# Gate and up columns of an expert layer: loaded per block from DRAM in place of copied from resident weights

## What is computed

```
x = x + xattn0(ctx_2048, layernorm(x), mask)        # 8 heads, 77 keys
x = x + moe0(layernorm(x))                          # 8 experts, top 2, I = 704, and one shared expert, 352
x = x + depool1(layernorm(x), ctx_2048, lengths)    # W_in, norms, a decaying sum over 77 patches, picked per row
x = x + moe1(layernorm(x))                          # 32 experts, top 6, I = 128, and one shared expert, 512
# moe0, per expert: silu(h @ Wg) * (h @ Wu) @ Wd, weighted by the softmax of the two best logits
```

## Time and profile before

| | us |
|---|---|
| median of 3 runs | 851.08 (849.27 to 855.88) |
| the profiled execution | 853.57 |
| its span, first to last instruction | 851.8 |
| TensorE busy | 741.3 |
| VectorE busy | 480.9 |
| ScalarE busy | 276.9 |
| GpSimd busy | 308.7 |
| mean granted TensorE clock | 0.93 of full |

### The profile page before, as it was taken

One profiled execution on the slowest core, in us unless ns is written; L12 is line 12 of the kernel. 1 busy time (PEld: TensorE's weight loads), 2 busy tenths in 40 slices (PEclk: granted clock), 3 DMA queues, 4 the chain that ended last, 5 costly groups with the idle time before them and its releaser, 6 DMA issues.

```text
span 851.8 us, 14479 instructions
## 1 busy us (share of the span) xinstructions
PE 741.3 (87%) x4703; PEld 644.3 (76%) x4703; DVE 480.9 (56%) x1694; ACT 276.9 (33%) x625; POOL 308.7 (36%) x328
## 2 busy tenths in 40 slices
PE   4989999979999999999989965898690899998875
PEld 3777778979999999999979944666460777777664
DVE  4997875226555555555535448788600455567663
ACT  2644432211111111111111123443330466665530
POOL 1332323730111111101101100777776377776750
PEclk9996887999999999999999975999996799999998
DMA  8970037442433443444330354766433666688966
GB/s 257 424 241 1 1 101 313 158 137 84 114 104 115 125 118 104 112 125 120 103 105 13 102 168 136 223 215 208 150 120 115 210 214 216 218 307 297 322 218 239
DMA packets 74516, 141.72 MB, mean 166 GB/s; under 512 B 8838, under 2 KB 53979, under 8 KB 73091
## 3 DMA queue, kind: packets, MB, share of 16 engines
q1 hardware_dynamic: 59036, 99.21, 38.0%
q0 software_dynamic: 13344, 38.68, 12.1%
q10 hardware_dynamic: 2046, 2.71, 1.1%
HBM read 93.34 MB, written 66.89 MB: 188 GB/s over the span
## 4 chain that ended last, share of the span: by engine, by line
PE 53%; POOL 15%; DVE 14%; issue 10%; DMA 4%; ACT 2%; DVEq 1%; SPq 0%; POOLq 0%; ACTq 0%
PE PB L603 21%; PE PB L629 12%; POOL rows_in L1921 8%; PE PB L818 5%; POOL sorted_x L1887 4%; POOL rows_out L1933 3%; PE PB L829 2%; PE PB L528 2%; DMA X<-in_x 2%; DVE WK L1797 1%; PE PB L696 1%; PE PB L804 1%; PE PB L582 1%; DVE WK L1282 1%; PE PB L860 1%
## 5 line engine op out<-in xcount | busy, mean ns | idle before, releaser
L603 PE MATMUL PB<-XT,UPW 128*128 128x128 f32 x1584 | 184.6, 277 | 3.4 <-DVE UPW L1454 3.1
L603 PEld LDWEIGHTS PB<-XT,UPW 128*128 128x128 f32 x1584 | 181.3, 193 | 3.8 <-DVE UPW L1454 3.3
L1896 POOL DMA_INDIRECT sorted_y<-WK x36 | 34.4, 955 | 267.1 <-DVE WK L1488 267.1
L1921 POOL DMA_INDIRECT rows_in<-XR,MB x96 | 93.1, 970 | 81.8 <-DVE MB L1687 53.2
L1454 DVE COPY UPW<-BIG 128x1024 f32 x72 | 64.3, 894 | 63.3 <-PE PB L603 37.4
L629 PE MATMUL PB<-BIG,WK 128*128 x432 | 99.2, 379 | 0.0
L629 PEld LDWEIGHTS PB<-BIG,WK 128*128 128x128 f32 x432 | 79.3, 190 | 9.3
L818 PE MATMUL PB<-XTB,WK 128*128 128x128 f32 x456 | 65.6, 288 | 14.0 <-DVE WK L1797 12.4
L935 ACT ACTIVATE XT<-PB 128x256 f32<-128x256 f32 x52 | 20.0, 384 | 171.0 <-PE PB L582 171.0
L818 PEld LDWEIGHTS PB<-XTB,WK 128*128 128x128 f32 x456 | 56.9, 196 | 22.9 <-issue 16.2
L1933 POOL DMA_INDIRECT rows_out<-WS,MB x58 | 57.5, 991 | 35.4 <-ACT WS L1074 22.6
(11 more groups left out here) (271 smaller groups left out, 1258.1 us busy)
## 6 DMA issues: line engine op xcount, KB each, us to landing
rows_in<-in_consts SPq DMA_DIRECT2D x32, 600.0 KB, 5.3
R<-rows_in SPq DMA_DIRECT2D x58, 300.0 KB, 3.9
BIG<-in_w SPq DMA_DIRECT2D x4, 2176.0 KB, 20.4
W1E<-in_w SPq DMA_DIRECT2D x32, 256.0 KB, 3.1
BIG<-in_w SPq DMA_DIRECT2D x1, 6528.0 KB, 19.3
sorted_x<-BIG SPq DMA_DIRECT2D x1, 5070.0 KB, 42.6
WK<-sorted_x SPq DMA_DIRECT2D x36, 130.0 KB, 2.3
XR<-rows_out SPq DMA_DIRECT2D x6, 768.0 KB, 8.2
```

The lines of the kernel that those rows point to most:

```text
L603: t = e.matmul(o[:, to:to + P], UPW[m][n % (m + 1)][:, k, c * P:(c + 1) * P], XT[:, n % 2, k, :], start=(k == 0), stop=(k == 1))
L1896: e.indirect_dma_start(out=DY, out_offset=bass.IndirectOffsetOnAxis(ap=DEST[:, i:i + 1], axis=0), in_=YS[:, i % 2, :], in_offset=None).the ...
L1921: e.indirect_dma_start(out=DX1, out_offset=bass.IndirectOffsetOnAxis(ap=SLOT1[:, i, j:j + 1], axis=0), in_=XR[:, i, :], in_offset=None).th ...
```

## The change

- BIG goes. One tile MEM is cut by hand. DW holds the down weights of all eight experts, loaded once at the start in two DMAs.
- Gate and up columns of a block are loaded by SyncE from the DRAM tensor in_w0 into UPW0 (now three buffers) and UPW1 (now two), at an address made from a register with the block's expert. VectorE's copies go.
- The attention's tiles, XNA, and the patches have room of their own, so the late loads of experts 4 to 7 go, and so do the store and the reload of the patches; the second layer reads DPA and SELA where they were made.
- The 32 clears of rows_in are queued on SyncE right behind the zeroing of sorted_x, in place of one per block.

```
-            for j in range(4):
-                e.dma_start(BIG[:, j, :], w0[j]).then_inc(*q.land("in_w", j))
+            for j in range(2):
+                e.dma_start(DW[:, 4 * j:4 * j + 4, :],
+                            w0[4 * j:4 * j + 4, :, 4 * I0:WE].rearrange("e p c -> p e c")).then_inc(*q.land("in_dw", j))
             q.wait_ge("set", "zero")
             e.dma_start(DX.rearrange("(n p) d -> p n d", p=P), ZERO.unsqueeze(1).broadcast_to([P, NBLK, RW0])).then_inc(
                 *q.land("zeroed"))
-            q.wait_ge("dpa", 3)
-            q.wait_ge("in_bin")
-            e.dma_start(DS[0], DPA.rearrange("k b d -> k (b d)")).then_inc(*q.land("spill", 0))
-            q.wait_ge("sel", 3)
-            e.dma_start(DS[1], SELA).then_inc(*q.land("spill", 1))
-            q.wait_ge("st", NT - 1)
-            q.wait_ge("spill", 1)
-            q.wait_ge("zeroed")
-            e.dma_start(BIG[:, 5:8, :].rearrange("p e c -> p (e c)"), w0[5:8].rearrange("e p c -> p e c")).then_inc(
-                *q.land("in_w5"))
+            for k in range(32):
+                e.dma_start(DX1[1 + 4 * P * k:1 + 4 * P * (k + 1), :].rearrange("(n p) d -> p n d", p=P),
+                            consts[:, NC_:NC_ + RW].unsqueeze(1).broadcast_to([P, 4, RW])).then_inc(*q.land("clear", k))
...
+            regs = {}
+
+            def up_weights(i, m, nb):
+                if i < nb:
+                    q.wait_ge("tab")
+                    if i not in regs:
+                        regs[i] = e.value_load(TAB[0:1, i:i + 1], min_val=0, max_val=E0 - 1)
+                    q.wait_ge(f"up{m}", EARLY + i - 3 + m if i >= 3 - m else -1)
+                    lo, hi = ((0, 7 * P), (7 * P, 11 * P))[m]
+                    e.dma_start(UPW[m][i % (3 - m)],
+                                w0[bass.ds(regs[i], 1), :, 0:4 * I0].rearrange("e p (k c) -> p (e k) c", k=2)[:, :, lo:hi]
+                                ).then_inc(*q.land(f"uw{m}{i % (3 - m)}", i))
 
             def block_iteration(n, nb):
-                last = EARLY + nb - 1
-                if n + 3 <= last:
+                if n + 3 < EARLY + nb:
                     fetch(n + 3, nb)
-                if n + 1 < EARLY and ((n + 1) % 4 == 3 or n + 2 == EARLY):
...
+                i = n - EARLY
+                if i < -1:
+                    return
+                if i == -1:
+                    up_weights(0, 0, nb)
+                    up_weights(0, 1, nb)
+                    up_weights(1, 0, nb)
+                else:
+                    up_weights(i + 1, 1, nb)
+                    up_weights(i + 2, 0, nb)
...
-                    e.tensor_copy(UPW[m][n % (m + 1)][:], BIG[:, bass.ds(regs[i], 1), 0:4 * I0].rearrange(
-                        "p e (k c) -> p (e k) c", k=2)[:, :, lo:hi]).then_inc(*q.mark(f"wc{m}", n))
...
-                        q.wait_ge(f"wc{m}", n)
+                        q.wait_ge(f"uw{m}{i % (3 - m)}", i)
...
-                e.dma_start(R16[0:KV + 1, 0:2048], DS[0]).then_inc(*q.land("in_dp", 0))
-                e.dma_start(SELT, DS[1]).then_inc(*q.land("in_dp", 1))
```

More of the change, by code:

```diff
@@ L335, in build @@
         ident = CC[:, CI:CI + P]
-        one = ExitStack()
         WS = sb("WS", [P, WSH])
         WK = sb("WK", [P, 5152])
-        BIG = alloc(one, "BIG", [P, E0, WE])
-        UPW = [[alloc(one, f"UPW{m}{k}", [P, 2, (7 - 3 * m) * P]) for k in range(m + 1)] for m in range(2)]
-        ROOM = BIG[:, 5:8, :].rearrange("p e c -> p (e c)")
+        MEM = sb("MEM", [P, 38624])
+        DW = MEM[:, 0:E0 * 6 * D].rearrange("p (e c) -> p e c", e=E0)
+        UPW = [[MEM[:, a + k * w:a + (k + 1) * w].rearrange("p (k c) -> p k c", k=2) for k in range(3 - m)]
+               for m, (a, w) in enumerate(((12288, 14 * P), (17664, 8 * P)))]
+        R16 = MEM[:, 19712:23808]
+        ROOM = MEM[:, 23808:36904]
         CX = ROOM[0:KV, 0:4096].rearrange("k (b d) -> k b d", b=B)
         A = ROOM[:, 4096:8320]
-        DPA = ROOM[0:KV + 1, 8320:10368].rearrange("k (b d) -> k b d", b=B)
-        SELA = ROOM[0:KV + 1, 10368:12416]
-        MB = ROOM[:, 12416:13032]
+        XNA = ROOM[:, 8320:12480].rearrange("p (t d) -> p t d", t=NT)
+        MB = ROOM[:, 12480:13096]
+        DPA = R16[0:KV + 1, 0:2048].rearrange("k (b d) -> k b d", b=B)
+        SELA = R16[0:KV + 1, 2048:4096]
         SS = WK[:, 0:2 * NH * KV].rearrange("p (a h k) -> p a h k", a=2, h=NH)
@@ L602, in up @@
                             for k in range(2):
-                                t = e.matmul(o[:, to:to + P], UPW[m][n % (m + 1)][:, k, c * P:(c + 1) * P],
+                                t = e.matmul(o[:, to:to + P], UPW[m][i % (3 - m)][:, k, c * P:(c + 1) * P],
                                              XT[:, n % 2, k, :], start=(k == 0), stop=(k == 1))
@@ L696, in attend @@
                             e.matmul(o, XP(i)[:, c, :], WIN[:, c, :], start=(c == 0), stop=False)
[L697 to L698 removed]
+                        q.wait_ge("dpa", 3)
+                        q.wait_ge("sel", 3)
+                        q.wait_ge("in_bin")
+                        e.matmul(o, SELA[:, i * P:(i + 1) * P], DPA[:, i // 2, :], start=False, stop=True).then_inc(
                             *q.mark("wi", i))
@@ L1437, in target @@
                         *q.mark("to", n))
[L1439 to L1445, removed]
-                            for j in range(4):
-                                q.wait_ge("in_w", j)
-                            q.wait_ge("in_w5")
-                            q.wait_ge("in_w4", 3)
-                        q.wait_ge("tab")
-                        regs[i] = e.value_load(TAB[0:1, i:i + 1], min_val=0, max_val=E0 - 1)
-                    lo, hi = ((0, 7 * P), (7 * P, 11 * P))[m]
-                    q.wait_ge(f"up{m}", n - m - 1)
-                    e.tensor_copy(UPW[m][n % (m + 1)][:], BIG[:, bass.ds(regs[i], 1), 0:4 * I0].rearrange(
-                        "p e (k c) -> p (e k) c", k=2)[:, :, lo:hi]).then_inc(*q.mark(f"wc{m}", n))
             def hidden(n, nb):
                 kind, i = item(n, nb)
-                weights(n + 1, 0, nb)
                 q.wait_ge("sg", n)
@@ L1496, in block_iteration @@
                     target(n + 1, nb)
-                    weights(n + 1, 1, nb)
                 if n < count:
```

61 lines of the change are left out of this document (20 added, 41 removed).

## The result

| | before | after |
|---|---|---|
| median of 4 runs, us | 853.48 (849.27 to 856.78) | 840.07 (839.12 to 842.64) |
| the profiled execution, us | 853.57 | 839.12 |
| its span | 851.8 | 837.3 |
| TensorE busy | 741.3 | 733.1 |
| VectorE busy | 480.9 | 419.2 |

The ratio of the two times is put at 0.9873, 95% interval 0.9832 to 0.9915: the change makes the kernel 7 to 14 us faster. (The two medians above, 13.4 us apart, have a ratio of 0.984, inside that interval too.) The forecast was 848.3 with a range of 844 to 854.

A forecast was written before the change was run, and what follows sets the result against it. TensorE's matmuls were taken as the bound, with the removed copies beside a full engine. Block 0's 3.0 us off the 851.08 median gave 848.1, rounded for the seams to 848.3, the other parts at zero; range 844 to 854.

The forecast's parts named there:

- Block 0: First expert block: weight loads replacing VectorE's copies start it at 188.6 to 189.5, not 191.70; gain 3.0 us taken.
- The steady blocks: Expert blocks stay 7.72 us apart; weights, rows and results stream at 221 GB/s, costed at nothing.
- The clears' end: Clears queued on SyncE behind the zeroing of sorted_x during attention would end near 143 us.
- Attention's first ten tiles: Attention beside the moved clears: a saturated DMA slows it by zero, with 2 us either way.
- (a): Weight stream comes late, L603 waiting in every block: 29 us more at 200 GB/s, so 877 us; chance 0.09.
- (b): Clears outrun attention, ending at 224; block 0 would wait 42 us: 890 us; chance 0.03.
- part 3: Patches stay in SBUF, two stores and two loads of 624 KB go: nothing on the path, seams 0, ends +1 and -1.
- Rival (c): Code comes late at the 437.63 branch behind queued weights: 3.81 us become 5 to 8, 849 to 852; chance 0.12.
- rival (d): TensorE's granted clock moves: a microsecond's shift can make or spare a slow stretch, 843 to 853; chance 0.11.

The follow-up runs named there:

- second pair of traces: The kernel before and the changed kernel each traced once more with no edit: 844.46 us and 838.53 us.

## Why the prediction was wrong

**Right.** Block 0: forecast a gain of 2.2 to 3.1 us, 3.0 taken; measured 2.5 in the distance from the last scatter and 2.6 from the first (1.9 in the second pair of traces). It is at the lower part because TensorE was free 0.3 us later than forecast, behind a wait of 2.24 us for block 0's rows (1.69 before), and then stood 0.30 us for the first load, which took 4.5 us where the sum had 3.9. The steady blocks: 243.17 us to the jump in both kernels; share 0.70 against a forecast of 0.6, 223 GB/s against 221. The clears' end: 143 forecast, 140 to 144 seen. Attention's first ten tiles are not slowed by the clears (last section). Rivals (a) and (b) didn't come, though the clears alone, in the kernel before, showed what (b) looks like, at a price of 7.4 us.

**The step that failed** is the end of part 3: "1.25 MB less ahead of the first seam and a fuller DMA at the second could give or cost about 1 us each; I take 0 for the pair, +1 and -1 as ends." ("First" is there the end of the layer, 498.53, and "the second" the jump into the copy, 437.63.) Measured: the jump -2.9 us, the gate and up behind it -1.6 (this term was in no sum, although has it at 6.80 us for 4.91), the layer's end -2.3 us, with +0.9 given back before rows_in: -5.8 us (-5.6 in the second pair of traces). With block 0 that is 8.4 us (7.5), where 3.0 was forecast. 853.57 - 8.4 = 845.2, still inside the range; from the median of 851.08 it is 842.7, below the range's low edge and 1% faster. The measured 840.07 lies lower still, and the part beyond the 8.4 us has no shown cause (below).

**Why.** I saw two gaps without a releaser and priced them at no change plus or minus one. Rival (c) named the right mechanism, that the jump waits for code behind queued data, and put the sign the wrong way round. I compared the megabytes per block, 1.44 against 0.6 queued. What counts is what is under way in the first microseconds behind the jump. Before, that was two clears of 600 KB, issued from 431.62 on: 1.2 MB and not 0.6. SyncE's timeline and a stretch of the kernel before:

```profile
431.62 1.33 SPq L2004 DMA_DIRECT2D rows_in<-in_consts  x2
```

```profile
435.00:437.00 2.00, 2.00 (x11) 1.77 (x10) 0.76 (x2) 0.00 (x0) 0.00 (x0) 1.00 0.98 246
```

In the changed kernel SyncE issues weights only as TensorE's gate and up releases a buffer; the last pair was issued from 420.64 on and had landed, the next left from 428.40 on. SyncE's timeline and a stretch of the changed kernel:

```profile
420.64 1.50 SPq L1964 DMA_DIRECT2D MEM<-in_w  x2
424.41 0.34 SPq L1953 DMA_DIRECT2D WK<-sorted_x  x1
428.40 1.83 SPq L1964 DMA_DIRECT2D MEM<-in_w  x2
```

```profile
428.00:430.00 2.00, 2.00 (x12) 1.77 (x12) 0.75 (x2) 0.00 (x0) 0.00 (x0) 1.00 0.40 103
```

The other seam lost its reload of 1.25 MB of patches, which the prediction named and then took as worth a microsecond at most.

**The clock behind the gap.** After 3.81 us of idle time TensorE ran at a granted clock of 0.57 from 442 to 446 us; after 0.91 us at 1.00 (columns: TensorE busy, clock, DMA share, GB/s; before, then changed).

```profile
442.00:446.00 4.00, 3.88 (x20) 0.57 0.00 0
```

```profile
432.40:436.40 4.00, 3.96 (x35) 1.00 0.65 234
```

So a longer wait for code costs twice (the gap, and the slow matmuls behind it), and what rival (d) says, "a shift of a microsecond can make or spare such a stretch", happened here, as a part of the gain.

**What is left over.** 14.5 us between the profiled executions less 8.4 are 6.1: attention 4.3 and the second layer 1.9, rounded. Both vary without the change: from the first reduction of attention to the first scatter the kernel before took 120.56 and 115.95 us, the changed one 117.35 twice, and with one clear per block again 122.36. In the first pair a part of it is a stretch of low clock that one execution has and the other not (before, then changed):

```profile
92.00:95.00 3.00, 3.00 (x16) 0.50 0.00 0
```

```profile
92.00:95.00 3.00, 3.00 (x20) 1.00 1.06 226
```

The medians differ by 13.4 us, and the interval of the ratio is 7 to 14 us: the 8.4 shown lie inside it. Whether the change also makes the low stretches rarer stays open. For it: attention took 117.35 to 117.7 us in all five traces of the changed kernel that have the clears behind the zeroing, and 115.95 to 122.36 in the other five, and the timed runs spread over 5 us (838 to 843) where those of the kernel before spread over 15 (843 to 858). Against the clears as its cause: moved alone, in the kernel before, they left attention at 120.57 us.

**What each part gave.** The stream: block 0's 1.9 to 2.6 us. The clears' move: the jump, since two clears per block in the kernel before gives the same 2.9 and 1.6 us, and two extra clears in the changed one take 3.3 and 1.2 back. But not alone: one clear per block beside the stream costs only 1.0 us at the jump. There the item's clear is issued at 435.98, behind its weight loads and behind the packet of code (435.5). The patches: the end of the layer, 2.3 us, as restoring them shows, of which 1.5 remain at the first scatter into rows_in.

## What to carry to other kernels

A gap behind a run-time jump in which the profile shows no releaser can be a fetch of code, and bulk transfers queued just ahead of it can raise its price: by 3.3 us here. Look in the DMA view for the instruction queue's packet, and keep bulk transfers that nobody needs out of the few microseconds around the jump. When work leaves a queue, price not only who waits for it but what else shares the DMA engines at that time. A term put at "about 1 us" either way beside a gap of 4 us must be bounded by the gap, with the slow clock behind it. And an edit that frees one wait can lengthen another: look at the whole trace before taking a seam's gain for the kernel's.

## What the runs showed of the hardware that was not expected

**Code waits behind data.** A 16 KB packet of code, about 1.0 us on its DMA engine (60.4% of 16 engines in 0.1 us), moved 1.0 us after the down step's start in the changed kernel, at a DMA share of 0.28, and 4.0 us after it with two extra clears queued, at a share of 1.08.

**Half a microsecond more of idle time, and the clock fell.** Block 0's gate and up took 5.02 us at a clock of 1.00 behind a wait of 3.10 us, and 6.65 us at a mean clock of 0.74 behind one of 3.58 us, with the same instructions on TensorE (the kernel before, and the same with two clears per block).

**A chip on which code came late beside the scatters.** On the chip where all kernels took some 977 us the blocks still came 7.72 us apart, but while GpSimd issued its scatters TensorE stood. The changed kernel there, a line of its timeline, and its waits from 140 to 220 us (us in total, times, longest):

```profile
157.03 0.37 PE L606 MATMUL PB<-XT,WS 128*128 128x128 f32 x1 [1.03 <-issue]
```

```profile
PE PB L619 <- issue: 12.8, 1, 12.8
PE PB L606 <- issue: 10.8, 11, 1.6
```

Its block 0 came 80.6 us behind the first scatter (49.1 on the first chip). Between 144 and 184 us no packet of an instruction queue moved, though the 16 engines were less than 40% busy from 140 to 180; on the first chip four moved in that stretch of the same program. Why that chip holds code back while scatters are under way was not found.

**A full DMA beside dense vector work.** In the changed kernel the loads, the zeroing and the clears keep the DMA engines at a share of 1.06 from 20 to 110 us; in the kernel before they rest from about 60 us on. From the first tile's reduction to the tenth's, up to about 72 us, attention took 53.0 us in both. Over all of attention a small cost can't be ruled out: the kernel before took 115.95 us at best, the changed one 117.35. Stretch of the changed kernel:

```profile
20.00:110.00 90.00, 82.30 (x519) 68.66 (x520) 82.81 (x220) 47.38 (x96) 32.22 (x37) 0.89 1.06 277
```
